# Routing tables moved to another DMA queue, layer norm steps gated by their place in an attention unit, and the third routing's one-hot columns issued one unit earlier

## The chip, the cores and the metric

The kernel runs on one core of one Trainium2 chip. The metric is the device time of one execution in microseconds; the median of three runs is given for the kernel before. All times inside the execution are read from one profiled execution of it.

## The reference

The program is one hybrid layer in float32, with x of 4 sequences x 1024 tokens x 256 channels:

```python
x = x + attn_a(layernorm(x))   # softmax(sin(angle/2)^2) mixes tokens, the same 1024x1024 matrix for all heads
x = x + ffn(layernorm(x))      # expert choice: 8 experts, each takes its 256 best tokens of each sequence
x = x + attn_b(layernorm(x))   # 16 heads of 64, causal, T = 1024
x = x + ffn(layernorm(x))      # the same gate and expert weights again

def ffn(x):                    # per sequence
    probs = softmax(x @ gate_w.T); g, m = top_k(probs.T, 256)
    h = gelu(x[m] @ w1) @ w2
    return zeros.at[m].add(g * h)
```

## The kernel before

Five programs, one per engine, run the same Python generator schedule, and each engine emits only its own instructions of a step. So the order of steps is the same on all engines, and inside one engine instructions run strictly in that order; semaphores tie the engines together. A `yield` in one generator lets another one advance (`pump`), and one advance is called a pump below.

**Stages.** Token mixing (0 to about 198 us) with the first routing woven in; 16 expert rounds of the first FFN (208 to about 620 us) with the second routing, the first norm and the first unit's projections woven in; 32 attention units (4 sequences x 8 head pairs, about 636 to 1795 us) with the third routing woven in; 16 expert rounds of the second FFN with the fourth routing woven in.

**A routing** (`route`, for pairs of sequences, r = 0 to 3; r = 2 is written out inside `attention`) takes probabilities, finds the 256th largest of each expert with ten count and digit steps, compares (`compare`), ranks on TensorE (`rank`, line 1249), and gets places (`positions`). Then for each of its two sequences it builds on VectorE a one-hot matrix A (`hot_digits`, line 2047), another one (`hot_places`, line 2054) and two columns C (`column`, line 2067); TensorE multiplies them (`table`, line 1267, 16 matmuls). `table_move` reduces the product to R on VectorE (lines 2078, 2081), and SyncE sends it with 8 small DMAs (line 2499) to `f_tab`. `indices` (lines 2088, 2089) waits on VectorE until all 8 have landed, and makes the row numbers `idx` and `row` from which GpSimd's gathers (line 2328) and scatters work. SyncE also stores the mixed rows (line 2453), in program order with the tables. TensorE takes the gathered tokens in `xin` (line 1280), then the experts' first products `up` (line 1299) and second products `down` (line 1320); between them ScalarE makes h (line 1664) and VectorE splits it into f_hhi and f_hlo (lines 2132, 2134), three rounds of slack behind.

**The last pieces of mixing.** TensorE's last products of the mixing stage go on until 197.8 us; VectorE adds them to x in `mix_residual` (line 1906), the last three after `indices` of the first routing.

**An attention unit** has 24 places (0 to 23), one per yield of `attend(u)`. TensorE does scores (lines 1411 and 1427), weighs values (line 1446), projects the next unit at places 0 to 7 (line 1348), and forms the next unit's row maxima (lines 1376, 1389) from place 6 on. VectorE reads these maxima from place 6 to 19 (lines 2180, 2186); TensorE transposes them at place 22 (line 1398), VectorE negates them into `t_neg` (line 2195), and a SyncE DMA puts them into `t_qb`, which the next unit's line 1427 waits for. ScalarE makes exp into t_p (line 1713), GpSimd masks it (line 2370), sums it (line 2390) and scales the result (line 2404). Line 1446 waits for GpSimd's mask on the diagonal blocks. The third routing is pumped at places 1, 5, 3 and 7, and at every place of the last unit, U-1 (31).

**Norms between sequences** (`between`): the rows of the last sequence and of the next one are normalized in the attention units, one step per pump at places 0, 2, 4, 6, 20 and 21: four statistics steps, one scale step (VectorE lines 1795 and 1798, then a GpSimd power at line 2253), and four row steps (lines 1805 and 1807). `prepare` of the next sequence runs whatever is left of it.

## Time and profile before

| | |
|---|---|
| median of 3 runs | 2235.77 us (2234.77 to 2235.8) |
| the profiled execution, its own time | 2237.5 us |
| its span, first to last instruction | 2235.8 us |
| TensorE busy | 2149.9 us (96%) |
| VectorE, GpSimd, ScalarE busy | 1465.4, 1368.7, 1003.6 us |
| mean granted TensorE clock | 0.987 |

TensorE is busy for nearly the whole span, so the time is read from its gaps: what it waited for, and where its clock was granted at less than full. The other engines matter where TensorE waits for them.

### The profile page before, as it was taken

How to read it: one execution, taken by the hardware profiler on the slowest of the kernel's cores; microseconds unless marked ns; L12 is line 12 of the kernel's file. 1: busy time of each engine (PE TensorE's matmuls, PEld its weight loads, DVE VectorE, ACT ScalarE, POOL GpSimd, SP SyncE). 2: the span in 40 equal slices, each digit the busy share in tenths (PEclk: the TensorE clock that was granted, in tenths of full speed). 3: DMA queues.
4: the chain of work that ended last, by engine and by line, in shares of the span. 5: the costliest groups of instructions: out<-in, count | busy, mean ns of one | idle time of the engine just before them, and what ended most of it. 6: DMA issues, size and time to landing. Idle time of an engine off the chain costs nothing.

```text
span 2235.8 us, 34077 instructions
## 1 busy us (share of the span) xinstructions
PE 2149.9 (96%) x12130; PEld 1597.8 (71%) x12130; DVE 1465.4 (66%) x3349; ACT 1003.6 (45%) x1907; POOL 1368.7 (61%) x1237
## 2 busy tenths in 40 slices
PE   6998999999999999999999999999999899999997
PEld 5455788889876666766657666667666588889997
DVE  6365688675757666467674577874877636975553
ACT  4411553444445545345553354542554425434443
POOL 2322676677537776566674576664677846777774
PEclk9899999999999999999999999999999999999999
DMA  4432544555432212212312222221220244545552
GB/s 132 144 129 86 151 117 111 151 144 137 114 88 67 51 36 76 67 52 73 76 48 67 67 78 56 58 61 54 76 76 21 76 132 115 140 113 139 134 144 29
DMA packets 145048, 206.04 MB, mean 92 GB/s; under 512 B 19432, under 2 KB 112112, under 8 KB 144880
## 3 DMA queue, kind: packets, MB, share of 16 engines
q1 hardware_dynamic: 120304, 170.30, 25.4%
q0 software_dynamic: 24576, 33.57, 8.8%
q8 instruction: 97, 1.59, 0.3%
q14 instruction: 71, 0.58, 0.1%
HBM read 130.03 MB, written 39.85 MB: 76 GB/s over the span
## 4 chain that ended last, share of the span: by engine, by line
PE 73%; DVE 9%; issue 4%; POOL 4%; ACT 2%; DMA 1%; SPq 1%; POOLq 0%; DVEq 0%; ACTq 0%
PE psum L1299 12%; PE psum L1320 11%; PE psum L1446 11%; PE psum L1348 7%; PE psum L1411 7%; PE psum L1427 6%; PE psum L1471 5%; PE psum L1362 4%; PE psum L1376 3%; PE psum L1456 3%; POOL t_acc L2390 2%; DVE f_hlo L2134 1%; DVE f_hhi L2132 1%; PE psum L1389 1%; PE psum L1267 1%
## 5 line engine op out<-in xcount | busy, mean ns | idle before, releaser
L1713 ACT ACTIVATE t_p<-psum 128x512 f32<-128x512 f32 (+3 forms) x768 | 323.6, 492 | 294.3 <-PE psum L1427 284.6
L2390 POOL TENSOR_TENSOR t_acc<-t_acc,t_p 128x1024 f32<-128x1024 f32 (+3 forms) x256 | 416.9, 1629 | 14.5 <-ACT t_p L1713 0.5
L2309 POOL TENSOR_TENSOR f_wlo<-f_wst,f_whi 128x256 fp32r<-128x256 f32 x256 | 221.8, 922 | 150.6 <-ACT f_whi L1646 150.6
L1320 PE MATMUL psum<-f_whi,f_hhi 128*128 128x256 f32 x1024 | 294.9, 288 | 6.2 <-DVE f_hlo L2134 6.1
L1446 PE MATMUL psum<-t_p,t_v 128*64 128x512 f32 (+3 forms) x1536 | 288.8, 496 | 7.3 <-POOL t_p L2370 7.3
L1320 PE MATMUL psum<-f_whi,f_hlo 128*128 128x256 f32 x1024 | 289.4, 283 | 0.0
L1320 PE MATMUL psum<-f_wlo,f_hhi 128*128 128x256 f32 x1024 | 289.2, 282 | 0.0
L2132 DVE CAST f_hhi<-f_h 128x512 fp32r<-128x512 f32 x256 | 141.9, 554 | 208.0 <-ACT f_h L1664 153.2
L1664 ACT ACTIVATE f_h<-psum 128x512 f32<-128x512 f32 x256 | 153.0, 598 | 275.8 <-PE psum L1299 246.8
L1411 PE MATMUL psum<-t_qa,t_ka 128*128 128x512 f32 (+3 forms) x768 | 222.7, 370 | 1.8 <-DVE t_mx L2180 0.6
L2390 POOL TENSOR_TENSOR t_acc<-t_p 128x768 f32<-128x768 f32 x64 | 134.6, 2103 | 136.4 <-PE psum L1456 133.1
L1446 PEld LDWEIGHTS psum<-t_p,t_v 128*64 128x64 f32 x1536 | 98.9, 137 | 161.8 <-issue 143.8
L2370 POOL TENSOR_SCALAR_AFFINE_SELECT t_p<-t_p 128x256 f32<-128x256 f32 x256 | 105.0, 420 | 175.0 <-ACT t_p L1713 174.5
L1299 PE MATMUL psum<-f_xhi,f_whi 128*128 128x512 f32 x512 | 204.8, 400 | 7.4 <-DVE f_xlo L2118 3.8
L1427 PE MATMUL psum<-t_qb,t_kb 65*128 65x512 f32 (+3 forms) x768 | 205.8, 349 | 4.9 <-DMA t_qb<-t_neg 4.5
L2134 DVE TENSOR_TENSOR f_hlo<-f_h,f_hhi 128x512 fp32r<-128x512 f32 x256 | 200.3, 783 | 8.8
L1320 PEld LDWEIGHTS psum<-f_whi,f_hhi 128*128 128x128 f32 x1024 | 194.9, 190 | 15.0 <-DVE f_hlo L2134 8.1
L1299 PE MATMUL psum<-f_xlo,f_whi 128*128 128x512 f32 x512 | 201.9, 394 | 0.0
L1299 PE MATMUL psum<-f_xhi,f_wlo 128*128 128x512 f32 x512 | 200.9, 392 | 0.0
L1320 PEld LDWEIGHTS psum<-f_wlo,f_hhi 128*128 128x128 f32 x1024 | 195.2, 191 | 4.8
L1320 PEld LDWEIGHTS psum<-f_whi,f_hlo 128*128 128x128 f32 x1024 | 195.0, 190 | 0.0
L2186 DVE TENSOR_REDUCE t_mx<-psum 128x1 f32<-128x512 f32 x256 | 159.6, 683 | 41.5 <-PE psum L1376 38.9
(288 smaller groups left out, 4408.1 us busy)
## 6 DMA issues: line engine op xcount, KB each, us to landing
f_wst<-in_L_ffn_w SPq DMA_DIRECT2D x64, 1024.0 KB
t_ka<-t_ka SPq DMA_DIRECT2D x64, 256.0 KB, 3.3
t_qb<-t_qa SPq DMA_DIRECT2D x64, 256.0 KB, 4.0
t_wk<-wkT SPq DMA_DIRECT2D x32, 256.0 KB, 4.0
t_wq<-wqT SPq DMA_DIRECT2D x32, 256.0 KB, 4.0
t_wv<-wvT SPq DMA_DIRECT2D x16, 512.0 KB, 4.9
normal<-f_xy SPq DMA_DIRECT2D x5, 1024.0 KB, 10.3
a_x<-in_L_attn_a_x SPq DMA_DIRECT2D x4, 1024.0 KB, 10.0
```

What stands on the lines that cost most here:

```text
L1299: m = pe.matmul(k.bank[b], w[:, dt, fs], x[:, dt, :], start=(dt == 0 and j == 0), stop=(dt == k.DT - 1 and j == 2))
L1320: m = pe.matmul(out, h[:, js], w[:, f, :], start=(f == 0 and a == 0 and j % 2 == 0), stop=(f == FT - 1 and a == 2), skip_group_check=True)
L1348: m = pe.matmul(k.bank[bank], w[:, part, ct, :], x[:, ct, cs], start=(ct == 0 and a == 0), stop=(ct == 1 and a == 2))
L1411: pe.matmul(k.bank[bank][:, q0:], hd["ka"][:, ks], hd["qa"][:, qs], start=True, stop=False)
L1427: pe.matmul(k.bank[banks[i]][:, q0:], hd["kb"][0:k.QROWS, ks], hd["qb"][0:k.QROWS, qs], start=False, stop=True).then_inc(k.filled[banks[i] ...
L1446: m = pe.matmul(k.bank[6][i * DH:(i + 1) * DH, q0:BANK], v[:, kt, vs:vs + DH], p[:, i, q0:BANK], start=(kt == 0), stop=(kt == last), skip_ ...
L1713: act.activation(p[:, i, q0:], k.bank[bank][:, q0:], ACT.Exp, scale=1.0 / float(np.sqrt(k.DH))).then_inc(k.drained[bank], 1)
L2132: dve.tensor_copy(hhi[:], h[:]).then_inc(k.d_h.sem, 1)
L2134: dve.tensor_tensor(hlo[:], h[:], hhi[:].bitcast(F32), ALU.subtract).then_inc(k.d_h.sem, 1)
L2186: s = dve.tensor_reduce(mx1[:, i, n - k.KPC:n - k.KPC + 1], part, AX.X, ALU.max)
L2309: m = pool.tensor_tensor(t["wlo"][n % 2][:, i, ks], t["wst"][:, i, ks], t["whi"][n % 2][:, i, ks].bitcast(F32), ALU.subtract)
L2390: pool.tensor_tensor(acc[:, :, q0:], (p0 if kt == 1 else acc)[:, :, q0:], p[:, :, q0:], ALU.add).then_inc(k.p_acc, 1)
```

## The change

- The first routing (r = 0) has its table DMAs issued by ScalarE; the other three keep them on SyncE.
- In all routings `indices` of the first sequence comes before `table_move` of the second on VectorE, and the marks of the semaphore follow that order. In r = 0 the second `table_move` comes two pumps later than before, and `indices` of the second sequence comes after the residual of block 6, whose successor (block 7) now follows it.
- In r = 1 the loads and norms begin three pumps sooner, the wait between sums and transposes is two pumps longer, and there is one more pump between `compare` and `rank`.
- The attention norms' scale step and first row step are emitted only at places 1 to 19 (pumps at 2, 4 or 6).
- In r = 2 the one-hot columns begin at place 10 of unit 30 instead of place 0 of unit 31, with one pump per place.

```diff
+        self.mix_residual(1, k.NBLK - 2)
+        self.mixed = True
+        yield
+        self.mix_residual(1, k.NBLK - 1)
...
-        yield
-        yield
-        yield
+        for _ in range(5 if r == 1 else 3):
+            yield
...
+        if r == 1:
+            yield
         self.rank(r, t)
...
         self.table_move(r, 0, pair[0], t)
         self.table(r, 1, t)
-        yield from steps(1, 3)
+        yield from steps(3, 3)
+        self.indices(r, 0, pair[0], t)
         self.table_move(r, 1, pair[1], t)
         yield
-        for i, b in enumerate(pair):
-            self.indices(r, i, b, t)
+        while r == 0 and not self.mixed:
+            yield
+        self.indices(r, 1, pair[1], t)
...
         if r == 1:
-            for _ in range(4):
-                yield
+            yield
...
+        def normalized(*args):
+
+            for n, _ in enumerate(self.norm(*args)):
+                yield
+                while n in (3, 4) and not 0 < state["place"] < 20:
+                    yield
+
         def prepare(b):
             if b:
+                state["place"] = 1
                 for _ in state["rows"]:
                     pass
...
             self.table(2, 1, early)
             yield from [None] * 2
+            self.indices(2, 0, 0, early)
             self.table_move(2, 1, 1, early)
             while not state["ended"]:
                 yield
-            for b in range(2):
-                self.indices(2, b, b, early)
+            self.indices(2, 1, 1, early)
...
-                    if u == U - 1 and place == 0:
+                    state["place"] = place
+                    if u == U - 2 and place == 10:
                         state["last"] = True
-                    if u == U - 1 or place in (1, 5) or place in (3, 7) and not state["busy"] or (
+                    if u == U - 1 or u == U - 2 and place > 9 or place in (1, 5) or place in (3, 7) and not state["busy"] or (
                             state["scored"] < 2 and place in (9, 11, 19, 23)):
                         pump(state["route"])
...
+    def table_move(self, r, i, b, t):
+        k, act = self.k, self.e
+        if r:
+            return
+        self.wait_ge(k.d_route.sem, k.d_route.at(r, ("R", i)))
+        for e in range(k.E):
+            act.dma_start(t["tab"][b][:, e].rearrange("q h t -> q (h t)"),
+                          t["R"][i][16 * e:16 * (e + 1), :]).then_inc(k.q_tab[i], DMA)
```

## Rows read from the trace of the kernel before

**Rows 1.** The page, part 4: shares of the chain that ended last.
```profile
PE 73%; DVE 9%; issue 4%; POOL 4%; ACT 2%; DMA 1%; SPq 1%; POOLq 0%; DVEq 0%; ACTq 0%
```
**Rows 2.** TensorE's waits: us in total, times, longest us.
```profile
PE psum L1446 <- POOL t_p L2370: 7.3, 5, 4.5
PE psum L1320 <- DVE f_hlo L2134: 6.1, 13, 1.0
PE psum L1427 <- DMA t_qb<-t_neg: 4.5, 2, 2.2
PE psum L1199 <- ACT f_wide L1606: 4.0, 3, 2.1
...
PE psum L1280 <- DMA f_xg<-normal,f_idx: 3.3, 2, 2.1
...
PE psum L1249 <- DVE f_ge L2009: 2.8, 2, 1.4
```
**Rows 3.** Timeline, first routing's tables: start us, duration us.
```profile
186.57 0.59 DVE L2081 TENSOR_REDUCE f_R<-f_junk 128x32 f32<-128x256 f32 x1
...
187.99 10.28 SPq L2499 DMA_DIRECT2D f_tab<-f_R  x16
...
194.40 0.17 DVE L2088 CAST f_idx<-f_tab 128x16 uint32<-128x16 f32 x1 [1.50 <-DMA f_tab<-f_R]
...
199.62 0.17 DVE L2088 CAST f_idx<-f_tab 128x16 uint32<-128x16 f32 x1 [4.97 <-DMA f_tab<-f_R]
```
**Rows 4.** Timeline of SyncE's queue, other issues around the tables.
```profile
186.23 1.71 SPq L2453 DMA_DIRECT2D res<-a_x  x2
...
200.55 0.33 SPq L2453 DMA_DIRECT2D res<-a_x  x1
```
**Rows 5.** VectorE's timeline, second routing's and fourth routing's indices.
```profile
400.62 0.17 DVE L2088 CAST f_idx<-f_tab 128x16 uint32<-128x16 f32 x1 [1.18 <-DMA f_tab<-f_R]
...
407.00 0.17 DVE L2088 CAST f_idx<-f_tab 128x16 uint32<-128x16 f32 x1 [6.13 <-DMA f_tab<-f_R]
...
2007.18 0.29 DVE L2088 CAST f_idx<-f_tab 128x16 uint32<-128x16 f32 x1 [3.71 <-DMA f_tab<-f_R]
```
**Rows 6.** VectorE's timeline at the end of attention unit 13.
```profile
1130.68 2.02 DVE L1807 TENSOR_SCALAR t_xy<-t_xy,t_mv,t_rstd 128x256 f32<-128x256 f32 x1
...
1133.24 0.24 DVE L2195 TENSOR_SCALAR t_neg<-psum 16x128 fp32r<-16x128 f32 x1
```
**Rows 7.** Windows: length, busy us of PE, PEld, DVE, ACT, POOL; PEclk, DMA, GB/s.
```profile
1136.00:1140.00 4.00, 4.00 (x16) 3.44 (x15) 1.91 (x5) 3.01 (x7) 1.51 (x3) 0.63 0.36 95
1436.00:1440.00 4.00, 3.71 (x12) 3.17 (x13) 3.37 (x9) 2.33 (x5) 1.84 (x4) 0.67 0.52 131
1764.00:1768.00 4.00, 1.44 (x4) 0.59 (x6) 0.94 (x1) 1.10 (x4) 3.82 (x5) 0.63 0.93 294
1768.00:1772.00 4.00, 4.00 (x12) 2.10 (x9) 0.00 (x0) 0.49 (x1) 3.79 (x4) 0.51 0.00 0
```
**Rows 8.** VectorE's timeline, end of unit 30 and start of unit 31.
```profile
1747.44 2.48 DVE L2186 TENSOR_REDUCE t_mx<-psum 128x1 f32<-128x512 f32 x4 [1.17 <-PE psum L1376]
...
1752.86 0.62 DVE L2180 CUSTOM_DVE_ANT_0 psum<-psum,t_mask,t_mx 128x384 f32<-128x384 f32 x1 [1.08 <-PE psum L1376]
...
1756.26 1.20 DVE L2047 TENSOR_TENSOR e_A<-e_hi,iota 128x1024 f32<-128x1024 int32 x1
...
1759.87 2.87 DVE L2067 TENSOR_TENSOR e_C<-e_hot,e_pr 128x1024 f32<-128x1024 f32 x1
1762.65 2.28 DVE L2047 TENSOR_TENSOR e_A<-e_hi,iota 128x1024 f32<-128x1024 int32 x1
```
**Rows 9.** Timelines of GpSimd and TensorE in unit 31.
```profile
1755.78 3.09 POOL L2370 TENSOR_SCALAR_AFFINE_SELECT t_p<-t_p 128x256 f32<-128x256 f32 x2
...
1766.01 0.76 POOL L2370 TENSOR_SCALAR_AFFINE_SELECT t_p<-t_p 128x256 f32<-128x256 f32 x2
...
1774.42 3.72 PE L1267 MATMUL psum<-e_C,e_A 128*128 128x256 f32 x16
```

More of the change, by code:

```diff
@@ L110, in semaphores @@
                              "key", "hi4", "lo4",
-                             *[(step, i) for i in range(2) for step in ("A", "hot", "C0", "C1")], ("R", 0), ("R", 1),
-                             ("idx", 0), ("row", 0), ("idx", 1), ("row", 1))
+                             *[(step, i) for i in range(2) for step in ("A", "hot", "C0", "C1")], ("R", 0), ("idx", 0),
+                             ("row", 0), ("R", 1), ("idx", 1), ("row", 1))
         self.pe_mixed = s("pe_mixed_gate")
@@ L531, in stage_a @@
                 self.mix_residual(1, i - 2)
-        for i in range(k.NBLK - 2, k.NBLK):
-            self.mix_residual(1, i)
+        self.mix_residual(1, k.NBLK - 2)
+        self.mixed = True
+        yield
+        self.mix_residual(1, k.NBLK - 1)
     def route(self, r):
@@ L682, in stage_f @@
         self.norm_of, self.routed, self.loaded, self.through = {}, -1, 0, 0
-        self.turned = 0
+        self.turned, self.mixed = 0, False
         first, second = iter(()) if layer else self.route(0), self.route(2 * layer + 1)
@@ L735, in attention @@
         early = t["early"]
-        state = dict(values=None, stored=0, rows=None, normal=0, scored=0, last=False, ended=False, busy=False)
+        state = dict(values=None, stored=0, rows=None, normal=0, scored=0, last=False, ended=False, busy=False, place=0)
         pairs = [(u, c, kt) for u in range(U) for c in range(NC) for kt in range(0, KPC * (c + 1), 2)]
@@ L748, in between @@
                 self.norm_of["out", b - 1] = self.runs
-                yield from self.norm(t["xy"], t["xy"], t["stats"], t["mv"], t["rstd"],
-                                     [(sem, DMA * b) for sem in k.q_xout])
+                yield from normalized(t["xy"], t["xy"], t["stats"], t["mv"], t["rstd"],
+                                      [(sem, DMA * b) for sem in k.q_xout])
                 state["normal"], state["busy"] = b, False
@@ L764, in between @@
                 self.norm_of["t", b + 1] = self.runs
-                yield from self.norm(t["xy"], t["xy"], t["stats"], t["mv"], t["rstd"], [(k.q_x, DMA * (2 + b))])
+                yield from normalized(t["xy"], t["xy"], t["stats"], t["mv"], t["rstd"], [(k.q_x, DMA * (2 + b))])
                 state["busy"] = False
+        def normalized(*args):
[3 more added lines that the diff above has]
+                    yield
         def prepare(b):
             if b:
+                state["place"] = 1
                 for _ in state["rows"]:
@@ L2496, in table_move @@
         k, sp = self.k, self.e
+        if r == 0:
+            return
         self.wait_ge(k.d_route.sem, k.d_route.at(r, ("R", i)))
```

## The prediction

> **What bounds the kernel now.** I read the page first, and there the chain that ended last: 73% of it is TensorE [rows 1], so the time is TensorE's work, its waits and the stretches at half clock. Next I read TensorE's waits [rows 2]; the rows that this change can touch are the masks of GpSimd (7.3 us in 5), the splits of VectorE (6.1 us in 13), t_neg (4.5 us in 2), the second and fourth routings' gate turns and ranks (4.0 and 2.8 us), and the first gathers (3.3 us). Then I read the timelines around each of these waits [rows 3 to 6, 8, 9] and the granted clock just behind them [rows 7]. The reader is to see that the edits do not change the amount of work at all. They move it in the in-order queues, so each part is priced as waits taken away, waits made later, and clock.
>
> **Part 1, the first routing's tables.** R of the first table ends at 186.57 + 0.59 = 187.16, but SyncE begins with the tables only at 187.99, since its two stores run until 187.94 [rows 3, 4]. The 16 DMAs take 10.28 us, 0.64 us each; the eighth starts at 192.5 and VectorE gets `idx` at 194.40, 1.9 us behind that start; the second `idx` is at 199.62. R of the second table had been there since 194.40 - 1.50 = 192.90 [rows 3].
>
> On ScalarE, which has nothing else there, the first eight can start at 187.2; at 0.64 us each the eighth starts at 191.7 and lands at 193.6. But now VectorE makes R of the second table only behind `idx` and `row` of the first: 193.9, and with 1.0 us for the two instructions (0.59 of it the row's) 194.9. Eight more DMAs: the last starts at 199.4 and lands at 201.3. That is 1.7 us later than 199.62, and TensorE's last wait for gathers [rows 2] is of the third and fourth gather, which hang on it. Earlier residuals (blocks 5 and 6 before the second wait) free two PSUM banks sooner, but the gathers end last there, so they give nothing. The part costs 1.7 us.
>
> No row has a DMA issued by ScalarE. Bounds are SyncE's shortest issue near by, 0.33 us, and its slowest, 1.71 / 2 = 0.85 us [rows 4]. With 0.33 us the second R is bound by TensorE's table as before (192.9), lands at 197.1, and the part gains about 2.2 us (the second gather must finish). With 0.85 us it costs 4.7 us. I take 0.64, the same transfer's own row. By the Trainium skill ("DMA: Bandwidth & Descriptors", "Issuing engines are not separate DMA queues") a second issuing engine saves issue time only and the transfers share the same DMA engines; no run here shows a ScalarE issue yet, and by that page nothing in the sum would change.
>
> **Part 2, indices ahead of the second table, r = 1 and r = 3.** Before, in r = 1, VectorE makes R of the second table while the first is in flight, gets the first `idx` at 400.62, and waits 6.13 us for the second until 407.00 [rows 5]. All h splits stand behind that wait. After, R comes behind the wait for the first: 400.6 + 0.3 + 1.0 = 401.9, and SyncE's eight with landing, 6.95 us as before, end at 408.9: 1.9 us later (before, SyncE had sent a weight load between and began behind it). TensorE already waits 1.0 us for f_hlo there (the longest of the 13 in [rows 2]), so nothing hides it: 1.9 us more, in one gap of 2.9 us. Gaps of 2.2 us were followed by a window at 0.63 and 0.67 of full clock, that is 1.5 and 1.3 us lost [rows 2, 7]: 1.4 us more. In r = 3 the second `idx` at 2007.18 [rows 5] comes 1.9 us later by the same steps; TensorE waits only 0.2 us there now, so the gap is 2.1 us and the clock is a coin toss: 1.9 + 0.7 = 2.6 us. Bounds: 0 (DMAs that land sooner) and 3.4 us each. For r = 2 the first landing is passed long before the sums behind it are due (four pumps, then the scores of the second chunk): nothing.
>
> **Part 3, the second routing's pumps.** One pump more between `compare` and `rank` puts an up or down product between them: the wait of rank for f_ge, 2.8 us in 2, is one of 1.3 to 1.4 us per routing, and one of the two goes: -1.3 us. Loads and norm three pumps sooner: the loads still wait for the third up product, so VectorE stands for them for a while, with the three rounds of slack as cover; without it the wait would be TensorE's. The power on GpSimd and ScalarE's norm rows then fall ahead of the next round's start instead of on it; and the second routing has the longest of the gate turn's waits, 2.1 us of the 4.0 [rows 2]. I take -1.5 us, most of one such wait; bounds -4 and +2 (a gate turn that meets a busier ScalarE). Parts 2 and 3 together: r = 1 gives 1.9 + 1.4 - 1.3 - 1.5 = +0.5, r = 3 +2.6.
>
> **Part 4, norms in a unit's middle.** At the end of unit 13 the first row step takes 2.02 us and stands ahead of t_neg, made at 1133.24 [rows 6]. TensorE then waits 2.2 us for it, and the same 300 us later: 4.5 us in 2, and 1.5 + 1.3 = 2.8 us of clock [rows 2, 7]. After, the scale step comes at place 2 of unit 14 (22), the row steps at 4 and 6, and the last two at place 20, where `prepare` runs the rest out. There they stand ahead of the transposes' splits, with short idle gaps of VectorE behind them to take them up. In the middle I price them 0.25 us a unit, with the next GpSimd power covered by its idle time; bounds 0 and 2.0 (one more colliding row step). Sum: -4.5 - 2.8 + 0.5 = -6.8 us; the norms after the out products already fall on places 2 and 4 and stay.
>
> **Part 5, the third routing's columns.** Now five one-hot steps run back to back on VectorE from 1756.26 to 1762.65 + 2.28 = 1764.93: 8.67 us, 1.73 us each, against 1.20 us alone [rows 8]. GpSimd slows with them: a pair of masks takes 3.09 us against 0.76 [rows 9]. TensorE waits for the masks (6.8 of the 7.3 us of [rows 2]), and loses 0.4 x 1.44 + 0.49 x 4.0, about 2.3 us with the end of it, at half clock [rows 7]: 9.1 us in unit 31. After, that unit has two steps instead of eight, and TensorE's second table product (about 3.5 us [rows 9]) covers GpSimd: I leave 1.0 us of wait.
>
> Unit 30 gets six of them between place 10 and place 22, where TensorE must have all maxima. VectorE's idle time there is 1.17 + 1.08 = 2.25 us [rows 8], and TensorE's first table product at place 20 gives it 3.5 us more. At 1.73 us each: 6 x 1.73 - 2.25 - 3.5 = 4.6 us of wait, and with a gap of that length 1.5 us of clock. So -9.1 + 1.0 + 4.6 + 1.5 = -2.0 us. Bounds: at 1.20 us each 1.5 us of wait, no clock, -7.1 us; at the slowest row, 2.87 us each, 11.5 + 1.5 us, and the masks late as before: +13.0 us.
>
> The Trainium skill ("SBUF — State Buffer", on the shared port pair) says that a VectorE instruction with two SBUF inputs and a GpSimd instruction reading SBUF exclude each other for whole instructions. The rows agree in kind, 3.09 against 0.76 us. GpSimd's adds fill most of unit 30's second half, so by that rule most of the six would wait out an add; this is the second rival.
>
> **Sum.** 1.7 + 0.5 + 2.6 - 6.8 - 2.0 = -4.0 us. Against the span, 2235.8 - 4.0 = 2231.8. The execution's own time is 1.7 us more than its span, while the median of the runs, 2235.77, stands at the span itself, so I predict 2231.8 for the median too. Within 0.2% (2231.3 to 2240.2) is about what a measurement cannot tell from no change.
>
> **The rivals.**
> 1. The collision only moves: unit 30's wait (4.6 + 1.5) stands, and unit 31 keeps most of its own, so part 5 gives +4: 2237.8. For it: GpSimd has no more idle time in unit 30 than in 31. Against: the steps are one per pump there, not in a row.
> 2. Slower: every step waits for an add on GpSimd, at the slowest row's 2.87 us, with the masks late as well. Part 5 is +13.0: 2235.8 - 2.0 + 13.0 = 2246.8. It decides from +6.5 in part 5: 1.8 us a step if unit 31 keeps all its wait, 3.1 us if it loses it as forecast. For it: the one step against a long add took 2.87. Against: the three before 1759.87 took 3.61 together.
> 3. ScalarE issues at 0.33 us, part 1 is -2.2: 2227.9. Nothing in the rows speaks for it but other shapes' issues.
> 4. Unit 30 hides the columns (1.20 us each): part 5 is -7.1, 2226.7.
> That the norm gate does nothing, since the rest piles up at place 20, gives 2238.6; the count of pumps speaks against it, and it is counted in rival 1.
>
> **Chances.** My forecast 0.42 (own range 2228.5 to 2235; 0.20 below 2231.3, 0.22 above), rival 1 0.17, rival 2 0.17, rival 3 0.16, rival 4 0.08. Faster 0.20 + 0.16 + 0.08 = 0.44; within 0.2% 0.22 + 0.17 = 0.39; slower 0.17. The range leaves out most of rival 2 and little below rival 4: 2225 to 2241.
>
> **What will show it.** Right: no wait for t_neg at the starts of units 14 and 22; second `idx` of the four routings some 1.7 to 1.9 us later behind its first R; a wait for f_hlo of about 3 us in r = 1; unit 30 longer and unit 31 shorter with a wait at line 1398 or for the banks of the maxima. Wrong: a ScalarE issue far from 0.64 us, one-hot steps in unit 30 far from 1.73 us, or a wait of the second unit that moves to line 1334's transposes. What would upset the whole most is unit 30, whose bounds are 20 us apart.

## The result and the profile after

The changed kernel takes 2244.26 us in the median of 7 runs (2242.45 to 2252.29), the kernel before 2235.77 us in 7 runs beside them (2232.95 to 2238.76). The two medians are 8.5 us (0.38%) apart; the ratio over all runs is 1.0047, 95% interval 1.0035 to 1.0058. So it is slower, where 4 us less was forecast, and lies beyond the range of 2225 to 2241. That rival 2's number (2246.8) is near is chance: it put +13 us on the third routing's columns, and that is not where most of the time went. The profiled execution's span is 2242.5 us at a mean granted clock of 0.985, 6.7 us more than before.

Its waits come first. TensorE's waits in the changed kernel, us in total, times, longest us:

```profile
PE psum L1333 <- DVE f_hlo L2156: 15.2, 14, 3.1
...
PE psum L1293 <- DMA f_xg<-normal,f_idx: 7.0, 3, 5.8
...
PE psum L1212 <- ACT f_wide L1619: 2.9, 3, 1.0
...
PE psum L1312 <- ACT f_h L1686: 2.4, 2, 2.0
PE psum L1459 <- POOL t_p L2392: 2.3, 1, 2.3
...
PE psum L1262 <- DVE f_ge L2031: 1.4, 1, 1.4
```

Against [rows 2]: the t_neg waits of 2.2 us are gone, the masks cost 2.3 in place of 7.3, one rank wait in place of two. But the h splits (f_hlo) cost 15.2 in place of 6.1, the first gathers 7.0 in place of 3.3, and there is a wait for h itself. Most of the new time is in the first FFN, and the largest part of it in the pumps of the second routing, which the forecast had put at -2.8 us.

Totals do not say where along the execution. For that I took the same instruction in both traces and subtracted its start times: the first gathered-token transpose of an expert round, and VectorE's t_neg. A step from one line of a column to the next is what that stretch costs. Before is in us, the others are differences to it. "After" and "again" are two profiles of the changed kernel; the other columns are kernels of the experiments below: the second routing's norm alone, the changed kernel with the second routing's edits or with the order of the indices taken back, and the gate or the columns alone.

| point | before | after | again | norm only | norm back | indices back | gate alone | columns alone |
|---|---|---|---|---|---|---|---|---|
| first FFN, round 2 | 226.78 | +2.00 | +2.17 | -0.42 | +1.51 | +0.10 | +0.65 | +0.63 |
| round 8 | 395.26 | +5.87 | +6.14 | +3.73 | +3.94 | +4.10 | +1.38 | +1.46 |
| t_neg for unit 0 | 623.18 | +9.46 | +7.45 | +4.68 | +7.00 | +5.11 | +1.53 | +1.68 |
| for unit 13 | 1097.62 | +10.07 | +8.30 | +4.76 | +7.86 | +5.76 | +1.97 | +1.66 |
| for unit 15 | 1165.40 | +8.22 | +7.90 | +3.33 | +7.33 | +5.55 | +0.11 | +1.70 |
| for unit 21 | 1397.81 | +8.21 | +7.92 | +3.35 | +7.38 | +5.60 | +0.17 | +1.76 |
| for unit 23 | 1467.42 | +6.23 | +6.12 | +3.64 | +5.51 | +3.93 | -1.63 | +2.01 |
| for unit 30 | 1728.05 | +6.11 | +5.99 | +3.69 | +5.30 | +3.79 | -1.79 | +2.03 |
| for unit 31 | 1756.05 | +13.50 | +13.37 | +3.69 | +12.69 | +11.18 | -1.79 | +9.40 |
| second FFN, round 1 | 1818.87 | +5.41 | +5.42 | +3.33 | +8.80 | +3.41 | -1.91 | +5.18 |
| round 8 | 2006.28 | +5.35 | +5.37 | +3.34 | +9.50 | +3.41 | -1.19 | +5.90 |
| round 9 | 2030.08 | +6.77 | +6.78 | +3.35 | +10.91 | +3.41 | -1.19 | +5.90 |

The changed kernel's column, added up: +2.0 to round 2, +3.9 to round 8, +3.6 to the first unit, +0.6 until unit 13, -1.85 and -2.0 around units 14 and 22, -0.1, then +7.4 in unit 30 and -8.1 behind it, and +1.4 in the fourth routing's indices.

Single steps of this table have to be read with care, since stretches that are the same in two kernels differ too. At round 2 the profiles of all kernels whose first routing is as before lie between -0.7 and +1.4. More than half of the changed kernel's +2.0 is of this kind: R of its first table, ahead of which nothing was edited, starts at 187.66, 1.1 us later than in [rows 3], and the mixing stage has had less clock (the kernel before, then the changed kernel):

```profile
40.00:80.00 40.00, 33.94 (x91) 14.99 (x90) 19.61 (x33) 24.12 (x33) 10.12 (x6) 0.74 0.02 7
40.00:80.00 40.00, 33.50 (x83) 14.09 (x82) 19.62 (x33) 23.83 (x33) 9.41 (x5) 0.70 0.02 7
```

The columns of numbers in such a line are length; busy us of PE, PEld, DVE, ACT, POOL; PEclk, DMA, GB/s. What a stretch loses to the clock is its length times what PEclk lacks to 1. Counted from that R, round 2 comes 40.2 us later in the kernel before, 39.8 to 40.7 in the profiles of all kernels with the old order in the first routing, and 41.1 to 41.2 in the three with the new one: the edits of the first routing cost TensorE 0.9 us.

**The +3.9.** ScalarE's timeline of the changed kernel, second expert round (start us, duration us; in brackets the idle time before and what ended it):

```profile
226.17 0.60 ACT L1686 ACTIVATE f_h<-psum 128x512 f32<-128x512 f32 x1 [1.30 <-PE psum L1312]
232.85 1.09 ACT L1540 ACTIVATE f_xy<-f_xy,f_rstd 128x256 f32<-128x256 f32 x2 [6.08 <-DVE f_rstd L1827]
...
234.79 0.58 ACT L1686 ACTIVATE f_h<-psum 128x512 f32<-128x512 f32 x1
```

VectorE, GpSimd and TensorE of the same stretch:

```profile
221.93 0.75 DVE L1808 BATCH_NORM_STATS2 f_stats<-f_xy 128x6 f32<-128x256 f32 x2 [2.45 <-DMA f_xy<-res]
...
235.40 0.57 DVE L2154 CAST f_hhi<-f_h 128x512 fp32r<-128x512 f32 x1 [1.94 <-ACT f_h L1686]
236.00 1.09 DVE L2156 TENSOR_TENSOR f_hlo<-f_h,f_hhi 128x512 fp32r<-128x512 f32 x1
...
230.03 2.59 POOL L2275 TENSOR_TENSOR f_rstd<-f_rstd,minus_half 128x8 f32<-128x8 f32 x1 [3.39 <-DVE f_rstd L1820]
...
237.15 0.38 PE L1333 MATMUL psum<-f_whi,f_hhi 128*128 128x256 f32 x1 [3.06 <-DVE f_hlo L2156]
...
255.44 0.50 PE L1312 MATMUL psum<-f_xhi,f_whi 128*128 128x512 f32 x1 [2.02 <-ACT f_h L1686]
258.33 0.66 PE L1188 MATMUL psum<-ident,f_xy 128*128 128x128 f32 x4 [1.23 <-ACT f_yT L1614]
```

Read it backwards from TensorE. Its 3.06 us wait ends with an h split at 236.00 + 1.09; the split waited for h on ScalarE at 234.79; and that activation stood behind a norm row step for which ScalarE had waited 6.08 us. The row step needs GpSimd's power (230.03 + 2.59), which needs the statistics, which waited 2.45 us for the load. SyncE issues that load at 216.43, before at 214.42, and round 2 starts 2.0 us later too: the load has not moved in its stage at all. In the kernel before ScalarE waits 4.51 us in the same step, but one h activation more (226.98) is already ahead of it. The clock falls behind the gap; windows of the changed kernel:

```profile
236.00:240.00 4.00, 2.85 (x14) 2.73 (x15) 4.00 (x8) 2.63 (x7) 3.54 (x5) 0.74 0.08 13
240.00:244.00 4.00, 4.00 (x17) 3.22 (x16) 2.09 (x7) 1.55 (x3) 3.09 (x4) 0.84 0.89 240
```

TensorE waited in these places in the kernel before too, but less:

```profile
237.39 0.50 PE L1299 MATMUL psum<-f_xhi,f_whi 128*128 128x512 f32 x1 [1.15 <-issue]
...
251.45 0.50 PE L1299 MATMUL psum<-f_xhi,f_whi 128*128 128x512 f32 x1 [1.16 <-ACT f_h L1664]
...
256.26 0.65 PE L1175 MATMUL psum<-ident,f_xy 128*128 128x128 f32 x4 [0.40 <-ACT f_yT L1601]
```

The three waits grow from 2.7 to 6.3 us, the clock takes 1.7 us (1.04 and 0.64 in the two windows), and the gate turn's wait (f_wide) is 0.95 us in place of 2.05. That is +4.2 us until round 4, and the +3.9 with -0.3 until round 8.

### The profile page after: what moved, and what is told of

Same layout as the page of the kernel before. It is cut to its first block, busy times and chain, and to the rows that moved or that the text cites. A ratio compares the mean times of both kernels' runs of the same rounds, so it can differ in the third digit from the quotient of the medians.

```text
span 2242.5 us, 34077 instructions
## 1 busy us (share of the span) xinstructions
PE 2153.5 (96%) x12130; PEld 1598.8 (71%) x12130; DVE 1464.6 (65%) x3349; ACT 1003.6 (45%) x1907; POOL 1373.8 (61%) x1237
## 4 chain that ended last, share of the span: by engine, by line
PE 72%; DVE 8%; POOL 4%; issue 3%; ACT 2%; DMA 1%; ACTq 0%; SPq 0%; POOLq 0%; DVEq 0%
PE psum L1312 12%; PE psum L1333 11%; PE psum L1459 11%; PE psum L1361 7%; PE psum L1424 6%; PE psum L1440 5%; PE psum L1484 5%; PE psum L1375 4%; PE psum L1389 3%; PE psum L1469 3%; POOL t_acc L2412 1%; PE psum L1402 1%; DVE f_hlo L2156 1%; DVE f_hhi L2154 1%; DVE f_wlo L2129 1%
## 5 line engine op out<-in xcount | busy, mean ns | idle before, releaser
L2331 POOL TENSOR_TENSOR f_wlo<-f_wst,f_whi 128x256 fp32r<-128x256 f32 x256 | 227.1, 953 | 153.5 <-ACT f_whi L1668 153.4
L1333 PE MATMUL psum<-f_whi,f_hhi 128*128 128x256 f32 x1024 | 296.2, 289 | 15.2 <-DVE f_hlo L2156 15.2
L2154 DVE CAST f_hhi<-f_h 128x512 fp32r<-128x512 f32 x256 | 136.4, 533 | 208.3 <-ACT f_h L1686 204.3
L2208 DVE TENSOR_REDUCE t_mx<-psum 128x1 f32<-128x512 f32 x256 | 159.6, 683 | 41.1 <-PE psum L1389 38.6
```

Of the source, the lines that this page charges most:

```text
L1333: m = pe.matmul(out, h[:, js], w[:, f, :], start=(f == 0 and a == 0 and j % 2 == 0), stop=(f == FT - 1 and a == 2), skip_group_check=True)
L2154: dve.tensor_copy(hhi[:], h[:]).then_inc(k.d_h.sem, 1)
L2208: s = dve.tensor_reduce(mx1[:, i, n - k.KPC:n - k.KPC + 1], part, AX.X, ALU.max)
L2331: m = pool.tensor_tensor(t["wlo"][n % 2][:, i, ks], t["wst"][:, i, ks], t["whi"][n % 2][:, i, ks].bitcast(F32), ALU.subtract)
```

## The experiments

Two to four kernels ran together on one chip, each with runs of the kernel before; medians are compared inside a group, and the table's positions carry the argument where the interval of the whole is too wide.

### The second routing's three edits

**All three taken back from the changed kernel, and all three alone.** The first:

```diff
-        for _ in range(5 if r == 1 else 3):
+        for _ in range(3):
...
-        if r == 1:
-            yield
         self.rank(r, t)
...
-            yield
+            for _ in range(4):
+                yield
```

> The changed kernel with the second routing's three pump edits taken back (loads and norm four pumps in, three pumps between sums and transposes, none extra ahead of rank). Theory A, the earlier norm costs: in the changed trace ScalarE stands 6.1 us in the norm's row step with an h activation behind it, TensorE waits 3.1 and 2.0 us, and its clock falls to 0.74 and 0.84 in the two windows behind; the starts of the expert rounds show +4.2 us from the second to the fourth round. Then this kernel takes 2244.3 - 4 to - 5 = 2239 to 2240.5 us, and the 3.1 us wait is gone. Theory B, the 4.2 us come from the later second idx of the first routing, which shifts all that follows against the engines: then this kernel stays at 2243 to 2245 us. What I forecast before (the edits gain 2.8 us) would give 2247.

> The kernel before with the second routing's three pump edits alone. Theory A: 2235.8 + 4 to 5 = 2239.5 to 2241 us, with a wait of TensorE for the h split of about 3 us near 235 us. Theory B (only together with the shifted first routing do they cost): 2234.5 to 2236.5 us. My forecast ahead of the result: 2235.8 - 2.8 = 2233.0 us.

Measured: taken back 2245.08 us against 2238.69, ratio 1.0024 (1.0014 to 1.0034), so half of the loss is gone; alone 2242.59 us, 1.0015 (1.0006 to 1.0024). The waits of 3.08 and 2.00 us stand in the one and not in the other, and they stand where the first routing is as before. Theory B falls. The table's column "norm back" shows less of the gain than the runs do: it is a profile of that kernel's longest run (2248.4 us), with a gate turn's wait of 2.81 us and 1.7 us of clock behind it between rounds 3 and 4, and with the slower of two outcomes in unit 31, told below.

**The norm alone, and the pump ahead of rank alone**, each with the wait behind the sums adjusted so that the rest stays. The first:

```diff
-            for _ in range(4):
+            for _ in range(1):
                 yield
...
-        yield
-        yield
-        yield
+        for _ in range(6 if r == 1 else 3):
+            yield
```

> The kernel before with the second routing's loads and norm alone three pumps sooner; six pumps in place of three between sums and transposes keep all that follows where it was. Theory A (the norm's row step stands on ScalarE ahead of an h activation while GpSimd makes the powers): waits of TensorE of about 3.1 us near 236 us and 2.0 us near 254 us as in the kernel with all three pump edits, and 5 to 5.5 us more than before at the start of the sixth expert round; in all +0.15 to +0.25%. Rival B (the sums and transposes one pump sooner, and the pump ahead of rank, are what costs): +0.05% or less, without these waits.

> The kernel before with one pump more between compare and rank of the second routing, taken from the wait between sums and transposes, so that compare and what precedes it come one pump sooner and rank stays where it was. My forecast: one of two waits for f_ge goes, -1.3 us, or -0.06%. Rival B: the wait goes, but a wait for the h splits near 350 us takes its place (1.5 and 0.8 us in the kernels with the edit): 0 to +0.05%.

Measured: the norm alone 2241.37 us against 2234.79, ratio 1.0027 (1.0018 to 1.0036). That is the mechanism of the changed kernel by itself: from round 2 to round 4 +4.2 us. That the norm alone stands at 1.0027 and the three edits together at 1.0015 is within the two intervals; nothing here explains a difference. ScalarE and TensorE of the kernel with the norm alone:

```profile
230.42 1.09 ACT L1526 ACTIVATE f_xy<-f_xy,f_rstd 128x256 f32<-128x256 f32 x2 [6.11 <-DVE f_rstd L1804]
...
234.73 0.39 PE L1319 MATMUL psum<-f_whi,f_hhi 128*128 128x256 f32 x1 [3.06 <-DVE f_hlo L2133]
```

The pump ahead of rank: 2234.76 us, 0.9997 (0.9988 to 1.0006). Its wait for f_ge goes, and two for h splits come in its place; the stretch from round 4 to 8 is 0.3 us shorter, not 1.3. TensorE in that kernel:

```profile
339.90 0.39 PE L1321 MATMUL psum<-f_whi,f_hhi 128*128 128x256 f32 x1 [0.78 <-DVE f_hlo L2135]
343.13 0.39 PE L1321 MATMUL psum<-f_whi,f_hhi 128*128 128x256 f32 x1 [1.55 <-DVE f_hlo L2135]
```

**The norm two pumps later instead**, alone and with the gate:

> The kernel before with the second routing's loads and norm two pumps later (six in place of four), and one pump in place of three between sums and transposes, so that what follows stays. Theory A, what counts is which h activation stands behind the norm's row step on ScalarE: two pumps later one more activation is ahead of the step, so the waits near 235 us (1.1 us) stay or shrink and none of 3 us appears; but the rows come two pumps later at the gate product: within 0.1% of the kernel before. Rival B, any shift of the norm costs, since the step then falls on another busy engine: +0.1 to +0.2%, with a new wait over 2 us between 230 and 290 us.

> The same later norm with the attention norms' gate on both steps, which alone stood at -0.10%. The sum of the two by theory A: -0.05 to -0.2%; by rival B: 0 to +0.1%.

Measured: 2241.26 us, ratio 1.0031 (1.0018 to 1.0043), and 2241.54 us, 1.0027 (1.0017 to 1.0038). By the total rival B holds, by the place it does not. Until round 4 the kernel is 0.6 us behind; then 5.3 us are lost at one point, which lies in what I had changed to keep the rest in place, one pump instead of three between sums and transposes:

```profile
293.19 0.66 PE L1229 MATMUL psum<-ident,f_wide 128*128 128x128 f32 x4 [3.09 <-DVE f_wide L1949]
```

So the later norm is cheap in its own stretch (round 2 to 3 takes 25.2 us, before 26.6, with the earlier norm 33.8), and the experiment as a whole measured its compensation. Whether another place would gain stays open.

### The order of the indices, and ScalarE's queue

**Both tables ahead of the first indices again, in the changed kernel; ScalarE's issue alone, in the kernel before.** The first:

```diff
-        yield from steps(3, 3)
-        self.indices(r, 0, pair[0], t)
+        yield from steps(1, 3)
         self.table_move(r, 1, pair[1], t)
         yield
-        while r == 0 and not self.mixed:
-            yield
-        self.indices(r, 1, pair[1], t)
+        for i, b in enumerate(pair):
+            self.indices(r, i, b, t)
...
```

The marks of the semaphore and the third routing's order are taken back with it, and so are the two extra pumps and block 7's place in the first routing: what each of these does by itself was not run.

> The changed kernel with the tables of both sequences ahead of the first indices again in all routings, and block 7's residual in its old place; ScalarE still issues the first routing's tables. Theory A: second idx in the first routing 2.5 us sooner (-2 us at the first up product), -2.8 us in the second routing, -1.4 us in the fourth, so about -6 us against the changed kernel (which stood at +0.47% to the kernel before), +0.2%. Rival B, the indices' order costs only where TensorE waits for f_hlo, and the waits move: -3 us or less, +0.35%.

> The kernel before with the first routing's table DMAs issued by ScalarE, order of steps as before. Theory A: the first eight start at R of the first table instead of 0.8 us later, so the first idx comes 0.8 us and the second 0.8 to 1.0 us sooner, -0.8 us, or -0.04%, in TensorE's wait for the third and fourth gather. Rival B: SyncE's stores and the tables now run at once and slow each other; the second idx comes no sooner: 0.

Measured: the order taken back 2241.02 us against 2234.79, ratio 1.0025 (1.0016 to 1.0034); with the changed kernel at 1.0047, on another chip, that is 5 us less. In the table its first step is +0.1 in place of +2.0 (40.1 us from R of the first table to round 2 in place of 41.1, so 1.1 us of it is the edit), from round 8 to unit 0 +1.0 in place of +3.6 or +1.3 (the two profiles of the changed kernel), and the fourth routing costs nothing in place of +1.4. The first, second and fourth routing, changed kernel:

```profile
187.66 0.59 DVE L2103 TENSOR_REDUCE f_R<-f_junk 128x32 f32<-128x256 f32 x1
...
194.73 0.17 DVE L2110 CAST f_idx<-f_tab 128x16 uint32<-128x16 f32 x1 [6.49 <-DMA f_tab<-f_R]
...
202.40 0.17 DVE L2110 CAST f_idx<-f_tab 128x16 uint32<-128x16 f32 x1 [5.15 <-DMA f_tab<-f_R]
...
406.58 0.18 DVE L2110 CAST f_idx<-f_tab 128x16 uint32<-128x16 f32 x1 [2.27 <-DMA f_tab<-f_R]
...
414.13 0.18 DVE L2110 CAST f_idx<-f_tab 128x16 uint32<-128x16 f32 x1 [6.32 <-DMA f_tab<-f_R]
...
415.59 0.55 PE L1333 MATMUL psum<-f_whi,f_hhi 128*128 128x256 f32 x1 [2.24 <-DVE f_hlo L2156]
...
2014.62 0.17 DVE L2110 CAST f_idx<-f_tab 128x16 uint32<-128x16 f32 x1 [5.26 <-DMA f_tab<-f_R]
...
2017.12 0.39 PE L1333 MATMUL psum<-f_whi,f_hhi 128*128 128x256 f32 x1 [1.57 <-DVE f_hlo L2156]
```

and with the order taken back:

```profile
404.84 0.17 DVE L2108 CAST f_idx<-f_tab 128x16 uint32<-128x16 f32 x1 [1.32 <-DMA f_tab<-f_R]
...
411.59 0.17 DVE L2108 CAST f_idx<-f_tab 128x16 uint32<-128x16 f32 x1 [6.49 <-DMA f_tab<-f_R]
...
413.04 0.36 PE L1331 MATMUL psum<-f_whi,f_hhi 128*128 128x256 f32 x1 [1.46 <-DVE f_hlo L2154]
```

The second routing's two indices are 7.55 us apart in the one and 6.75 in the other (6.38 in [rows 5]), and TensorE's gap is 2.24 against 1.46 us. The same gap of 2.24 us stands in three profiles: behind it the clock took 1.7 us in the changed kernel's first profile and in the one with the second routing's edits taken back, and nothing in the changed kernel's second; that is most of the 2.3 us between +3.6 and +1.3.

ScalarE's issue alone: 2235.39 us, 1.0000 (0.9992 to 1.0009). Its timeline against [rows 3]:

```profile
186.94 0.59 DVE L2090 TENSOR_REDUCE f_R<-f_junk 128x32 f32<-128x256 f32 x1
...
187.57 10.83 ACTq L1634 DMA_DIRECT2D f_tab<-f_R  x16
...
192.67 0.60 DVE L2090 TENSOR_REDUCE f_R<-f_junk 128x32 f32<-128x256 f32 x1
...
194.05 0.17 DVE L2097 CAST f_idx<-f_tab 128x16 uint32<-128x16 f32 x1 [0.78 <-DMA f_tab<-f_R]
...
199.65 0.17 DVE L2097 CAST f_idx<-f_tab 128x16 uint32<-128x16 f32 x1 [5.35 <-DMA f_tab<-f_R]
```

Counted from R of the first table, the first indices come 7.1 us behind it in place of 7.8, the second 12.7 in place of 13.05: 0.7 and 0.3 us sooner. The second eight transfers wait for R of the second table (192.67 + 0.60; the ninth starts at 193.30), so little of the earlier start is left for them. Neither of my expectations named that. The 0.3 us is too little for the runs to show.

### The norms' gate

**Both steps gated, alone in the kernel before; and the row step alone**, so that GpSimd's power stays in the unit before. The second differs from the first in one line:

```diff
-                while n in (3, 4) and not 0 < state["place"] < 20:
+                while n == 4 and not 0 < state["place"] < 20:
                     yield
```

> The kernel before with the attention norms' gate alone. Read from the changed trace: units 14 and 22 are shorter by 1.85 and 1.98 us, so 2235.8 - 3.9 = 2231.9 us (theory A). Rival B, my forecast for this part, -6.8 us: 2229.0 us, if the 2.7 and 3.7 us by which the two units still exceed a unit without a norm come from other edits. Rival C, the units' gain is given back by a later wait: 2235.8 us.

> The kernel before with a gate on the first row step of the attention norms alone; the scale step stays at place 20 of the unit before, so GpSimd's power no longer falls among the adds at the start of the next unit. In the kernel with both steps gated the wait for t_neg (2.2 us and 1.5 us of clock) was gone from units 14 and 22, but two new waits stood there, 0.8 us for GpSimd's t_acc and 0.5 us for a split of VectorE, and the units were 1.8 us shorter each. Theory A, the power causes the wait for t_acc: that wait goes, units 14 and 22 are 2.6 us or more shorter each, in all -5 us, or -0.15 to -0.25%. Theory B, the row steps at places 4 and 6 cause both: as with both gated, -1.8 us each, -0.10 to -0.15%.

Measured: both steps 2236.92 us against 2238.69, ratio 0.9990 (0.9981 to 0.9999); the row step alone 2233.94 against 2234.92, 0.9998 (0.9989 to 1.0007). The t_neg wait is gone in both, and the wait for t_acc stays without the power, so theory A of the second run falls. TensorE and GpSimd in unit 14, kernel with the row step gated:

```profile
1144.59 0.61 PE L1398 MATMUL psum<-t_ka,t_qa 128*128 128x256 f32 x2 [0.84 <-POOL t_acc L2399]
...
1142.43 2.15 POOL L2399 TENSOR_TENSOR t_acc<-t_acc,t_p 128x512 f32<-128x512 f32 x2
```

and the window it lies in:

```profile
1144.00:1148.00 4.00, 3.38 (x12) 1.46 (x14) 3.15 (x13) 0.69 (x2) 1.21 (x2) 0.60 0.34 108
```

GpSimd's add ends at 1144.58 and TensorE starts at 1144.59. With the 2.2 us gap ahead of it gone, TensorE catches up with GpSimd in the same unit, waits 0.84 us, and now the clock falls here, to 0.60, in place of [rows 7]. Over all nine profiled kernels with the gate, the two stretches (t_neg for unit 13 to 15, and 21 to 23) are 0.2 to 1.9 us and 1.6 to 2.0 us shorter than in the profile of before; without the gate they already vary, from 1.5 us shorter to 1.5 us longer for the first, and the 2.2 us wait for t_neg stands in each of them. Means of the nine profiles with the gate and of the nine without it, in us (waits over 0.3 us):

| | t_neg for unit 13 to 15 | waits of TensorE in it | lost to the clock | for unit 21 to 23 | waits | lost to the clock |
|---|---|---|---|---|---|---|
| without the gate | 67.2 | 2.3 | 0.9 | 69.9 | 2.7 | 1.9 |
| with the gate | 67.1 | 1.2 | 1.3 | 67.8 | 0.9 | 1.7 |

So the gate gains 0.1 us around unit 14 and 2.0 us around unit 22, 2.1 us in all, which is what the runs of the gate alone show. It takes waits away and no clock.

### The third routing's columns

**Alone; from place 16 in place of 10; and this with the row step's gate:**

```diff
-                    if u == U - 1 and place == 0:
+                    if u == U - 2 and place == 10:
                         state["last"] = True
-                    if u == U - 1 or place in (1, 5) or ...
+                    if u == U - 1 or u == U - 2 and place > 9 or place in (1, 5) or ...
```

> The kernel before with the third routing's columns one unit sooner alone. Theory A, read from the changed trace: unit 30 +7.4 us, unit 31 -8.7 us, net -1.3: 2234.5 us, and the wait for GpSimd's masks in unit 31 falls from 6.8 to about 2.3 us. Rival B: the net stands only because the rows of unit 30 were moved by the norm gate; alone the part costs +4: 2240 us. Rival C, the slowest row for each step: 2248 us.

> The kernel before with the third routing's columns from place 16 of unit 30 on, not from place 10: two or three one-hot steps ahead of the maxima's last reads and the other five or six behind t_neg. Theory A, each step costs what GpSimd's instruction beside it costs, wherever it stands: unit 30 +3 us, unit 31 about -2 us, +1 us or +0.05%, between the kernel before and the one from place 10 on (+0.10%). Theory B, the steps fit into the idle time of unit 30 if they are few: unit 30 +1 us, unit 31 -3 to -5 us, -0.10 to -0.15%.

> The kernel before with both of these: the row step's gate, and the columns from place 16 of unit 30. The two act in different units, so the sum of the two is expected: -4 us or -0.18% by theory A of both; if the whole is off the sum by more than 2 us, the collisions of unit 30 and 31 depend on the phase that the gate leaves.

Measured: alone 2241.95 us against 2238.69, ratio 1.0010 (1.0001 to 1.0019); from place 16 on 2238.97 against 2234.92, 1.0017 (1.0008 to 1.0026); with the gate 2237.96, 1.0013 (1.0004 to 1.0022), which is the sum of its parts within their intervals. Both are worse than either theory had: the columns from place 16 at most +0.05%, the two together -0.18%. Fewer steps ahead of t_neg do not help: the fourth falls just ahead of it, and TensorE waits 2.83 us for t_neg where before it waited for nothing.

With the start at place 10 unit 30 costs +7.4 us in all five profiled kernels, but what follows until the second FFN is -8.1, -8.0 and -7.8 us in three of them and -4.2 and -3.9 in two. Unit 31 of the changed kernel, VectorE and GpSimd:

```profile
1769.75 1.20 DVE L2089 TENSOR_TENSOR e_C<-e_hot,tokid 128x1024 f32<-128x1024 f32 x1
1770.89 1.21 DVE L2089 TENSOR_TENSOR e_C<-e_hot,e_pr 128x1024 f32<-128x1024 f32 x1
...
1769.56 4.24 POOL L2412 TENSOR_TENSOR t_acc<-t_acc,t_p 128x768 f32<-128x768 f32 x1
```

and of the kernel with the second routing's edits taken back:

```profile
1768.95 2.70 DVE L2088 TENSOR_TENSOR e_C<-e_hot,tokid 128x1024 f32<-128x1024 f32 x1
1771.57 2.29 DVE L2088 TENSOR_TENSOR e_C<-e_hot,e_pr 128x1024 f32<-128x1024 f32 x1
...
1768.75 1.81 POOL L2411 TENSOR_TENSOR t_acc<-t_acc,t_p 128x768 f32<-128x768 f32 x1
...
1774.24 0.69 PE L1423 MATMUL psum<-t_qa,t_ka 128*128 128x384 f32 x1 [2.34 <-DVE e_Rw L2099]
...
1776.00:1780.00 4.00, 4.00 (x13) 3.43 (x13) 0.00 (x0) 1.32 (x5) 3.53 (x6) 0.50 0.37 85
```

The same instructions in the same order: in one kernel GpSimd's add takes 4.24 us and the columns 1.20 and 1.21, in the other the add takes 1.81 and the columns 2.70 and 2.29. One of the two engines stands. When it is VectorE, the product's R comes late, TensorE waits 2.34 us for its bank, and its clock falls to half; that is the 4 us between the two groups. The add's record starts 0.19 us ahead of the column in the one and 0.20 us in the other, so the records do not tell which goes first. In all five profiles the lead is 190, 191 and 195 ns where the add stands, and 199 and 204 ns where the column does; whether so small a difference decides was not tested.

In unit 30 TensorE waits once, for the maxima, and its clock takes 1.7 us (changed kernel):

```profile
1751.90 1.10 PE L1424 MATMUL psum<-t_qa,t_ka 128*128 128x512 f32 x2 [1.66 <-DVE t_mx L2208]
```

**Later instead of sooner**: the columns from place 8 of unit 31, one pump apart; and this with both gated steps; beside them the changed kernel a second time.

```diff
-            yield from [None] * 2
+            yield
             self.hot_places(2, 0, early)
...
-                    if u == U - 1 and place == 0:
+                    if u == U - 1 and place == 8:
                         state["last"] = True
```

> The kernel before with the third routing's columns later, not sooner: they begin at place 8 of unit 31, one pump apart, behind VectorE's first wait for TensorE in that unit. Theory A, the loss is whose instruction a step meets on GpSimd: at the start of unit 31 they meet the masks that TensorE waits for (waits of 2.0 and 2.0 to 4.5 us and 2.3 us of clock), later they meet adds that nobody waits for; then both waits for t_p at the start of unit 31 go, waits of 1 to 3 us at its end may grow since the adds end later: -3 to -6 us, or -0.15 to -0.25%. Theory B, any 8 steps of 1.2 to 2.9 us in unit 31 cost the same, since GpSimd is full in it: 0, within 0.05%.

> The same later columns with the attention norms' gate on both steps. Sum of the two: 0.1% below the run with later columns alone, so -0.25 to -0.35% by theory A, -0.1% by theory B.

> The changed kernel as it is, a second time. Theory A, the last two one-hot columns fall on either side of one add of GpSimd's by a difference of 0.2 us: its times spread over 5 us or more, and this profile shows either two steps of 1.2 us at the start of unit 31 or two of 2.3 to 2.7 us with a wait of 2.3 us for e_Rw behind them. The waits of 3.1 us and 2.0 us in the second and third expert round stand as before, within 0.1 us. Ratio +0.35 to +0.58%. Rival: those waits vary between executions too.

Measured: 2235.97 us against 2235.17, ratio 1.0001 (0.9992 to 1.0010); with the gate 2234.47, 0.9998 (0.9989 to 1.0007); the changed kernel 2246.29, 1.0054 (1.0040 to 1.0067). In the later columns' profile the longest mask wait shrinks to 2.0 us, but a wait for the column itself appears, and the clock falls all the same. TensorE in unit 31:

```profile
1758.28 0.44 PE L1446 MATMUL psum<-t_p,t_v 128*64 128x128 f32 x4 [2.02 <-POOL t_p L2370]
...
1774.61 3.69 PE L1267 MATMUL psum<-e_C,e_A 128*128 128x256 f32 x16 [2.21 <-DVE e_C L2067]
```

From unit 31 to the second FFN it is 1.0 us shorter than before. Two steps still run at the start of the unit (1755.62 and 1756.75), where VectorE waits for nothing. With the gate the same stretch is 0.2 us shorter. Theory A is not refuted, but its gain is 1 us or less and not 3 to 6. The changed kernel's second profile repeats the waits of 3.06, 2.08, 5.66 and 1.57 us and lands within 0.01 us of the first at the second FFN, though its runs too spread over 4.8 us. It again shows the two columns on the cheap side; the other side was not seen in a profile of this kernel.

## Why the prediction was wrong

Forecast by parts, and what the runs show in its place:

- **Part 1, +1.7: right for the indices, half of it for TensorE.** The second indices come 14.7 us behind R of the first table in place of 13.05, 1.7 us later, as worked out, in all three profiles with the new order. ScalarE's DMAs took 0.55 to 0.67 us each, the row of SyncE that I took; rival 3 (0.33 us) falls. But TensorE loses only 0.9 us: its waits for the gathered tokens come to 7.05 us in place of 3.3 + 2.8, where the 2.8 is a wait for a PSUM bank that the residuals hold. The prediction had said of the earlier residuals that "they give nothing"; that wait is gone in the three profiles and stands, at 2.4 to 3.2 us, in all others. +2.0 in the table looks right by luck, since 1.1 us of it had passed before the first table.
- **Part 2: mechanism right, sizes near.** From round 8 to unit 0 the three profiles with the new order show 1.3 to 3.6 us against 3.3, those with the old order -0.2 to +1.0. The gap is 2.24 us in place of 2.9, since the sum counted R of the second table twice: the 6.95 us "as before" run from the start of R (393.67 to 400.62), and R's own 0.6 us stands in the 1.0 us added ahead of them. So the indices are 1.2 us farther apart, not 1.9. The clock behind the gap fell in two profiles of three. In the fourth routing +1.4 in place of 2.6, a gap of 1.57, with no fall.
- **Part 3, -2.8: this step failed, by 6.7 us.** It said: "VectorE stands for them for a while, with the three rounds of slack as cover". VectorE did stand, 2.45 us. But the cover was counted for what is queued behind that wait on VectorE. The norm has row steps on ScalarE as well, behind GpSimd's power; the prediction named them as falling well, "ahead of the next round's start", and put no wait on them. Behind them stands the next h activation. The three rounds of slack did not cover it: TensorE waited 3.1, 2.0 and 1.2 us where it had waited 1.15, 1.16 and 0.4, and the clock took 1.7 us more. The -1.5 us for the gate turn was drawn from a 2.1 us wait. In the ten profiles of kernels with the old pumps it is 0.95 us in six and 2.8 in three: a term that does not repeat. The -1.3 us for rank went to h splits but for 0.3.
- **Part 4, -6.8: the waits right, the clock wrong.** The two waits of 2.2 us went as forecast. The clock behind them, priced at 2.8 us from one window each (over 12 us behind the wait it is 1.7 us each, 3.4 in all, in the kernel before), did not come back: in the mean of nine profiles each, the two stretches lose 2.8 us to the clock without the gate and 3.0 with it, behind new waits of 0.5 and 0.8 us. And the price left in the units, 0.25 us each, was too small, so that the waits shrink by 2.9 us in all and not by 4.0. Together -2.1 us, not -6.8. The first profile's -3.8 is partly luck, since the clock did not fall in its unit 14, as in two of the nine.
- **Part 5, -2.0: near in three of five profiles, by two misses that offset each other.** Unit 30 was to cost 4.6 us of wait and 1.5 of clock beside the table product moved into it; it costs 1.7 and 1.7, and with the product's 3.7 us it is 7.4 us longer. Unit 31 was to give back 8.1 us beside the product and gives back 4.4: the waits for masks fall from 6.5 to 2.3 us, but one of 0.85 us for t_neg is new, the last for GpSimd's t_yT grows by 0.6, and of the clock 1.8 us come back. So the clock only moved from one unit to the other. In the other two profiles the part is +3.2 and +3.5, which is rival 1, "the collision only moves", at +4. Rival 2 falls, the part being far from +13; so does rival 4, for the unit did not hide the columns. The six one-hot steps in unit 30 took 1.18 to 2.65 us, 1.70 in the mean, against 1.73 taken. Two of its numbers were off: the clock in unit 31 was 3.4 us between 1764 and 1776 and not 2.3, and the -7.1 of rival 4 adds up to -6.6. And the 1.20 us "alone" is a step beside GpSimd's masks, whose record runs from 1755.78 to 1758.87 [rows 8, 9]: it is the length of a step that does not stand.

The Trainium skill ("SBUF — State Buffer", "SBUF: two separate sides") says that of a VectorE operation with two SBUF inputs and a GpSimd operation that reads SBUF the one that starts first has the shared ports for its whole length and the other is blocked. The rows of unit 31 agree: 4.24 us is 1.81 + 1.20 + 1.21 and 0.02 more. What no run here shows is who wins.

No version beats the kernel before by more than 0.1%: the gate alone is the best, at 0.9990 with an upper limit of 0.9999. The changed kernel's loss is the norm's place (+0.27% by itself), the order of the indices (5 us when taken back) and the columns (+0.10% by themselves), less the gate.

## What to carry to other kernels

A step that is pumped sooner has to be followed through every engine on which it issues. An early norm whose load comes no sooner only parks its row step in ScalarE's queue, and what counts is the single activation that now stands behind it, not the average slack. When a 2 us gap is taken away, look at once for what TensorE catches up with in the next 10 us; here all of the clock that the gate was to give back went there, and a third of the waits. And one wait's length in one profile is not a price: two profiles of kernels equal up to that point differed by 1.9 us at the same wait. Nor is one step of a table of start times: look first whether the two profiles already differ ahead of the edit, and whether the step is one loss of clock.

## What the runs showed of the hardware

- Between two kernels with the same order of instructions there a pair of one-hot columns took 1.20 + 1.21 us or 2.70 + 2.29 us, and GpSimd's add beside them 4.24 or 1.81 us. A total 4 us apart hung on that.
- Clock losses came in like sizes. Behind the same wait of 2.2 us for t_neg in unit 14, the nine profiles without the gate lost 0 us (five of them), 1.7 us (three) or 3.4 us (one) to the clock. The mixing stage lost 10.3 or 12.0 us between 40 and 80 us in kernels that are equal there. A clock loss behind a gap of 2 us has to be carried as a range, and two profiles 1.7 us apart may be the same kernel.
- ScalarE issued 16 small DMAs in 10.83 us, of which 0.5 us is a pause for the second R: one each 0.65 us, beside SyncE's 0.64.
